# A vision tower on one core: scores in four 32-row quarters over four PSUM banks, and the norm weight of the last stage applied when turned gelu rows are evicted

## The chip, the core and the metric

The kernel runs on one core of one Trainium2 chip, in one launch. Its engines, each with its own queue of instructions in program order, are TensorE (PE, with its weight loads shown as PEld), VectorE (DVE), ScalarE (ACT), GpSimd (POOL) and SyncE (SP, which issues DMAs). Matrix products land in PSUM, eight banks of 512 float32 per partition, and are read from there by VectorE and ScalarE. The metric is the device time of the launch in microseconds, the median of several runs; lower is better.

## The reference

32 images of 96 x 96 x 3 are cut into 36 patches of 16 x 16 x 3; with two class tokens there are S = 38 tokens of D = 256 features. Then four residual blocks:

```python
h = patches @ W.T + b, class token, pos_embed; second class token in front
h = h + attn0(ln(h))       # 16 heads of 16, rope, causal softmax, @ Wo.T
h = h + moe(ln(h))         # 8 experts, top 2: sum_e gate_e * (x @ w_in[e].T @ w_out[e].T)
h = h + attn1(ln(h))       # 16 heads, no mask; every head's weights applied to 8 retrieval values,
                           #   a softmax over the 8 mixes them; @ Wf.T; then ln, relu MLP 256-512-256
h = h + ffn(ln(h))         # below
```

```python
h = x @ absmean(W_fc).T            # ternary weights: -1, 0, 1; 256 -> 1024
h = gelu(h)
h = layernorm(h, ln_w, ln_b)       # (h - mu) * rsqrt(var + eps) * ln_w + ln_b
return h @ absmean(W_proj).T       # ternary, 1024 -> 256
```

## The kernel before

The 1216 tokens are worked in T = 11 tiles of R = 114 rows (G = 3 images of 38 tokens); the last tile overlaps the one before. Every tile goes through four stages: a (patches, first attention), c1 (gate and experts), c2 and c3 (second attention and its MLP), d (the ternary block: d0 and d1 norm and first product, d2 gelu norm and projection). All order is written out by hand, engine by engine: straight lists of calls such as `c2_scores(2)`, and three hardware loops. The loop of stage a runs t = 2 to 7 and also multiplies each expert's two matrices together (`combine`). The middle loop runs `c_step(i)` for i = 5 to 10 and works on five tiles at once: c1 of i and i - 1, c2 of i - 2, the mixing of i - 3 and c3 of i - 4. The last loop runs `d_step(i)` for i = 4 to 10 with up to four tiles in hand; before it stands a straight list of what is left of c2 and c3 for tiles 9 and 10, with the first d calls between. Engines wait for each other through semaphores (`wait_ge`), each engine in its own order.

Precise products: an operand is split into a high part in float32r (one pass of the array) and a low part, the remainder; `mm3` (L1806 to L1810) multiplies high x high, high x low and low x high. So an eviction of a turned operand is a ScalarE copy to the high part (`turn_hi`, `d2_hi`) and a VectorE subtraction to the low part (`turn_lo`, `d2_lo`). Where one side is exact in the high part, as ternary weights are, two products do (`d1_fc`, L2163 and L2164). The projection of stage d has `ln_w` multiplied into its weights ahead of the loop (`proj_hi`, `proj_lo`: `pw_h`, `pw_l`), so it needs three (L2184); the mean is taken off by `ncs`, the column sums of those weights (`proj_sums`), and `ln_b` goes in by `bw` (`proj_bias`).

Scores of all 16 heads of three images are computed by block structure: `q_exp` holds q of one image with zeros around it, `k_exp` holds k of every head of a group in its 16 rows and zeros elsewhere, built by VectorE with the mask `hmask` (`a1_k`, `c2_k`, L1038 and L1264). Rows 0 to 63 and 64 to 127 of the array work on different banks of `score` (L1873). The softmax takes a maximum over both banks (L1044), subtracts it (L1050), takes three exps (L552), and `turn_p` (L1891) turns the 16 weights of 114 x 114 in four groups into two banks, `tb[0]` and `tb[1]`; ScalarE (L560), in stage a also VectorE (L1059), evicts each group to `pt`, and the group after next waits for that.

PSUM before: `bank0` to `bank2`, two banks of `score`, `tb0`, `tb1`, `bz`. The two `tb` banks also take turned x2, q and k, the products for q, k and v of stage c2, the output projection of stage a and, in stage d, the projection.

## Time and profile before

| what | value |
|---|---|
| median of three runs | 553.65 us (553.48 to 555.54) |
| profiled execution | 550.58 us, of which the span of the profile is 548.8 |
| granted TensorE clock over the span | 0.993 of full speed |
| instructions | 12145 |
| middle loop (six turns) | 289.8 to 415.7 us |
| from there to the end | 133.1 us |

The profile is one execution. Busy times of a group may overlap its neighbours; a record's duration is longer than its spacing from the next, since products are pipelined. A float32 product shows as two records, each of all its columns. A waiting time counts only where the waiting engine is the bound.

### The profile page before, as it was taken

To read this page: it belongs to the slowest core of one execution; us is meant where nothing else is said; L and a number is where in the kernel's file an instruction comes from. 1 tells how busy PE (TensorE), PEld (TensorE's weight loads), DVE (VectorE), ACT (ScalarE), POOL (GpSimd) and SP (SyncE) were. 2 spreads that over 40 slices of the span, in tenths; PEclk is the share of its full clock that TensorE was granted. 3 is DMA by queue.
4 is the path that set the end of the run, shared out by engine and by line. 5 is a ranking of instruction groups with operands and counts; after the bars stand their busy time and mean duration, and the time that the engine had idled before them with its cause. 6 is when DMAs were issued, how large, how long until landed. Compare 5 with 4: busy or idle time off the path is not lost.

```text
span 548.8 us, 12145 instructions
## 1 busy us (share of the span) xinstructions
PE 506.9 (92%) x3902; PEld 426.6 (78%) x3902; DVE 375.6 (68%) x943; ACT 272.9 (50%) x634; POOL 190.5 (35%) x257
## 2 busy tenths in 40 slices
PE   8989999999998878989999999999999989889996
PEld 7878877887877656667778888888888768678885
...
DMA packets 10990, 29.62 MB, mean 54 GB/s; under 512 B 2192, under 2 KB 3408, under 8 KB 10704
## 3 DMA queue, kind: packets, MB, share of 16 engines
...
q8 instruction: 17, 0.28, 0.2%
q14 instruction: 13, 0.11, 0.1%
...
## 4 chain that ended last, share of the span: by engine, by line
PE 42%; DVE 6%; issue 5%; ACT 3%; POOL 1%; DVEq 1%; POOLq 0%; ACTq 0%
PE score L2069 6%; PE tb L1808 3%; PE score L1873 3%; PE bz L2099 3%; PE tb L1810 3%; PE tb L1809 3%; PE bank L1810 3%; PE bank L1809 3%; PE bank L1808 3%; PE tb L1891 2%; PE bz L2081 2%; PE bz L1822 1%; PE bz L1808 1%; DVE we_h L1438 1%; PE tb L1822 1%
## 5 line engine op out<-in xcount | busy, mean ns | idle before, releaser
L383 POOL TENSOR_TENSOR h<-h,scaled 114x256 f32 (+1 forms) x88 | 69.1, 785 | 49.9 <-ACT scaled L686 43.3
L335 POOL TENSOR_TENSOR small<-small,half 114x1 f32<-114x1 f32 x44 | 25.8, 586 | 136.5 <-DVE small L969 136.5
L552 ACT ACTIVATE p_exp<-sc,cst 114x608 f32<-114x608 f32 x66 | 48.2, 795 | 25.6 <-DVE sc L1050 25.6
L1923 PE MATMUL bz<-ebuf 128*128 128x256 f32 x256 | 58.7, 382 | 0.0
L560 ACT ACTIVATE pt<-tb 114x456 f32<-114x456 f32 x66 | 34.6, 556 | 36.0 <-PE tb L1891 36.0
L1923 PEld LDWEIGHTS bz<-ebuf 128*128 128x128 f32 x256 | 47.7, 192 | 5.9
L1891 PE MATMUL tb<-cst,p_exp 114*114 114x114 f32 x352 | 44.0, 266 | 6.1 <-ACT pt L560 3.3
L2069 PE MATMUL score<-v,pt 114*114 114x137 f32 x352 | 48.9, 282 | 0.3 <-ACT o L653 0.3
L686 ACT ACTIVATE scaled<-bank,gl 114x256 f32<-114x256 f32 x88 | 39.0, 473 | 17.3 <-PE bank L1810 6.2
L1891 PEld LDWEIGHTS tb<-cst,p_exp 114*114 114x114 f32 x352 | 35.2, 134 | 15.1 <-ACT pt L560 6.7
L2069 PEld LDWEIGHTS score<-v,pt 114*114 114x114 f32 x352 | 44.1, 178 | 2.1 <-issue 0.4
L1873 PE MATMUL score<-k_exp,q_exp 64*114 64x152 f32 x528 | 40.6, 298 | 0.9 <-DVE k_exp L1264 0.8
L1873 PEld LDWEIGHTS score<-k_exp,q_exp 64*114 64x114 f32 x528 | 35.2, 175 | 7.0 <-issue 6.9
L1808 PE MATMUL bank<-we_h,xth 128*114 128x512 f32 x88 | 38.2, 434 | 0.1
L1809 PE MATMUL bank<-we_l,xth 128*114 128x512 f32 x88 | 35.0, 398 | 0.0
L1810 PE MATMUL bank<-we_h,xtl 128*114 128x512 f32 x88 | 34.9, 397 | 0.0
L346 POOL TENSOR_TENSOR o<-o 114x512 f32<-114x512 f32 x11 | 14.0, 1274 | 59.5 <-DVE o L1030 59.5
L653 ACT ACTIVATE o<-score 114x411 f32<-114x411 f32 (+1 forms) x66 | 31.2, 480 | 2.9 <-PE score L2069 2.0
L509 ACT ACTIVATE xth<-bank 128x228 fp32r<-128x228 f32 x33 | 11.8, 358 | 35.8 <-PE bank L1822 35.8
L1808 PE MATMUL tb<-wa,we_h 128*114 128x256 f32 x88 | 25.7, 292 | 2.5 <-DVE we_h L1438 2.1
L1044 DVE TENSOR_REDUCE smax<-score 114x16 f32<-114x608 f32 x22 | 17.3, 786 | 13.0 <-PE score L1873 12.9
L757 ACT ACTIVATE we_h<-score 128x456 fp32r<-128x456 f32 x22 | 11.1, 550 | 28.5 <-PE score L2175 28.5
...
## 6 DMA issues: line engine op xcount, KB each, us to landing
...
```

The costliest lines, as they stand in the source:

```text
L383: gp.tensor_tensor(h[0:R, t, :], h[0:R, t, :], scaled[0:R, e % 4, :], ALU.add).then_inc(moe_acc, 1)
L552: act.activation(p_exp[0:R, :, b * S:(b + 1) * S], sc[0:R], ACT.Exp, bias=cst[0:R, CB + b:CB + b + 1], scale=SCALE).then_inc(exps, 1)
L560: act.activation(pt[0:R, 4 * g:4 * g + 4, :], tb[g % 2][0:R, 0:4 * R].rearrange("p (h r) -> p h r", h=4), ACT.Copy).then_inc(pt_odd if g % ...
L653: act.activation(o1[0:R, h0:h0 + k, :], score[0:R, g % 2, 0:k * VE].rearrange("p (h d) -> p h d", h=k), ACT.Copy).then_inc(pv1_out, 1)
L686: act.activation(scaled[0:R, e % 4, :], bk[1 + e // 2 % 2][0:R, (e % 2) * D:(e % 2 + 1) * D], ACT.Copy, scale=gl[0:R, 7, e:e + 1]).then_in ...
L1808: pe.matmul(dst, lh, rh_, start=first, stop=False)
L1809: pe.matmul(dst, lh, rl_, start=False, stop=False)
L1810: return pe.matmul(dst, ll, rh_, start=False, stop=last)
L1873: last = pe.matmul(score[0:R, i, f * HQ * S:(f + 1) * HQ * S], q_exp[rows64, f].rearrange("p b x -> p (b x)")[:, b * R:(b + 1) * R], k_exp ...
L1891: last = pe.transpose(tb[g % 2][0:R, i * R:(i + 1) * R], p_exp[0:R, 4 * g + i, :], cst[0:R, CI:CI + R])
L1923: last = pe.matmul(bz[:, m * D:(m + 1) * D], ebuf[:, 0, c * D + m * P:c * D + (m + 1) * P], ebuf[:, 1, c * D:(c + 1) * D], start=(c == 0 a ...
L2069: last = pe.matmul(score[0:R, g % 2, i * VE:(i + 1) * VE], pt[0:R, place(h0 + i), :], v1[0:R, :], start=True, stop=True)
```

## The change

Scores. `score` has four banks; `tb[0]` and `tb[1]` are now its third and fourth. The head groups are halved (HQ = 2), `k_exp` and `hmask` are half as wide, and a score call has 24 products of 76 columns on four groups of 32 rows, each into its own bank, in place of 12 of 152 on two groups of 64. The causal mask is written by four products of 152 columns instead of two of 304. Maximum and subtraction read four banks with the same number of elements and operations. Since a score call overwrites `tb`, the output projection of stage a goes to the second half of `bank2` (but for the last tile), with waits on that bank's other reader, and in c2 the v product comes ahead of q and k.

Last stage. `d2_hi` multiplies by `ln_w` as it copies, one operation per chunk of 128 hidden units (the weight is then a value per partition): 8 of 114 columns instead of 2 of 456. `d2_lo` does the same with a multiply and subtract, 8 instead of 2. The projection uses the ternary weights themselves and needs two products per chunk. `proj_hi`, `proj_lo`, `lnw_halves` and `lnw_low` are gone; the column sums are computed in float32 from `ln_w` spread over 114 columns (`weight_wide`, `proj_sums`).

Order. The lists of all engines are written anew, and the last loop is written out, call by call, between what is left of c2 and c3.

```diff
     f, i, j = h // HF, h % HF // HQ, h % HQ
-    return i * HF + f * HQ + j
+    return i * HB + f * HQ + j
 
 
...
-        score = ctx.enter_context(nc.psum_tensor("score", [P, 2, 512], F32))
-        tb = [ctx.enter_context(nc.psum_tensor(f"tb{i}", [P, 512], F32)) for i in range(2)]
+        score = ctx.enter_context(nc.psum_tensor("score", [P, 4, 512], F32))
+        tb = [score[:, 2 + i, :] for i in range(2)]
+
+        def wo_place(t):
+
+            return tb[0][0:R, 0:D] if isinstance(t, int) and t == T - 1 else bk[2][0:R, D:2 * D]
...
-                    act.activation(gth[:, 4 * q:4 * q + 4, :], score[:, q, 0:4 * R].rearrange("p (c r) -> p c r", c=4),
-                                   ACT.Copy).then_inc(gT_hi, 1)
...
+                    for c in range(4):
+                        k = 4 * q + c
+                        last = act.activation(gth[:, k, :], score[:, q, c * R:(c + 1) * R], ACT.Copy, scale=lnwc[:, k:k + 1])
+                    last.then_inc(gT_hi, 1)
...
-            s = score[0:R, :, 0:HF * S].rearrange("p f (h j) -> p f h j", j=S)
+            s = score[0:R, :, 0:HB * S].rearrange("p f (h j) -> p f h j", j=S)
...
-                    V.tensor_tensor(sc[0:R, f * HF:(f + 1) * HF, :], s[:, f],
-                                    smax[0:R, f * HF:(f + 1) * HF].unsqueeze(2).broadcast_to([R, HF, S]),
-                                    ALU.subtract).then_inc(shifted, 1)
+                    two_banks = slice(2 * f * HB, 2 * (f + 1) * HB)
+                    top = smax[0:R, two_banks].rearrange("p (i h) -> p i h", i=2)
+                    V.tensor_tensor(sc[0:R, two_banks, :].rearrange("p (i h) j -> p i h j", i=2), s[:, 2 * f:2 * f + 2],
+                                    top.unsqueeze(3).broadcast_to([R, 2, HB, S]), ALU.subtract).then_inc(shifted, 1)
...
+            def weight_wide():
+                dve.wait_ge(pt_mm, 8 * T)
+                dve.wait_ge(lnw_in, 16)
+                V.tensor_copy(lnwr, lnwc[:].unsqueeze(2).broadcast_to([P, HC, R])).then_inc(widened, 1)
...
-                V.tensor_scalar(ncs[0:R], tb[0][0:R, 0:D], -1.0, None, ALU.mult).then_inc(bw_ready, 1)
+                V.tensor_scalar(ncs[0:R], tb[1][0:R, D:2 * D], -1.0, None, ALU.mult).then_inc(bw_ready, 1)
...
-                    V.tensor_tensor(gtl[:, 4 * q:4 * q + 4, :], score[:, q, 0:4 * R].rearrange("p (c r) -> p c r", c=4),
-                                    gth[:, 4 * q:4 * q + 4, :].bitcast(F32), ALU.subtract).then_inc(gT_lo, 1)
+                    for c in range(4):
+                        k = 4 * q + c
+                        last = V.scalar_tensor_tensor(gtl[:, k, :], score[:, q, c * R:(c + 1) * R], lnwc[:, k:k + 1],
+                                                      gth[:, k, :].bitcast(F32), ALU.mult, ALU.subtract)
+                    last.then_inc(gT_lo, 1)
...
+                since(dve, done, t)
+                dve.wait_ge(g_stat, 4 * t + 4)
...
             def a1_v(t):
                 since(pe, v0_ready, t)
+                since(pe, res0, t - 1)
...
-                    for i in range(2):
-                        pe.matmul(score[0:R, i, 0:HF * S], idb[0:R, 0:R], cmask[0:R], start=True, stop=False)
+                    for i in range(4):
+                        pe.matmul(score[0:R, i, 0:HB * S], idb[0:R, 0:R], cmask[0:R], start=True, stop=False)
...
-                        for i in range(2):
-                            rows64 = slice(i * P // 2, (i + 1) * P // 2)
+                        for i in range(4):
+                            rows32 = slice(i * P // 4, (i + 1) * P // 4)
                             last = pe.matmul(score[0:R, i, f * HQ * S:(f + 1) * HQ * S],
-                                             q_exp[rows64, f].rearrange("p b x -> p (b x)")[:, b * R:(b + 1) * R],
-                                             k_exp[rows64, f, :, b * S:(b + 1) * S],
+                                             q_exp[rows32, f].rearrange("p b x -> p (b x)")[:, b * R:(b + 1) * R],
+                                             k_exp[rows32, f, :, b * S:(b + 1) * S],
                                              start=(not causal and b == 0),
...
                 pe.wait_ge(oT_lo, t + 1)
-                product(tb[0][0:R, 0:D], xth[1], xtl[1], wa, A_O, D, (0, D)).then_inc(wo_mm, 1)
+                pe.wait_ge(v0_ready, min(t + 2, T) if isinstance(t, int) else t + 2)
+                product(wo_place(t), xth[1], xtl[1], wa, A_O, D, (0, D)).then_inc(wo_mm, 1)
...
             def c2_v(t):
-                pe.wait_ge(q_ready, 2 * (t + T) + 2)
+                pe.wait_ge(t2["lo"], t + 1)
                 product(tb[0][0:R, 2 * R:2 * R + W2], xth[1], xtl[1], wc, C_V, W2, (0, W2)).then_inc(v1_mm, 1)
 
             def c2_qT(t):
                 pe.wait_ge(qk1_out, t + 1)
+                pe.wait_ge(v1_ready, 2 * t + 2)
                 turned(tb[0][:, 0:2 * R], qk_rows[:, 0:D]).then_inc(qkT1_mm, 1)
...
             def c_step(i):
+                c2_pv(i - 3, (0, 1))
                 c2_x(i - 2)
-                c2_pv(i - 3, (0, 1))
                 c3_att(i - 4)
-                c2_pv(i - 3, (2, 3))
+                c2_pv(i - 3, (2,))
                 c3_wf(i - 4)
+                c2_pv(i - 3, (3, 4))
+                c1_moe(i - 1, (2,))
+                c2_pv(i - 3, (5,))
+                c2_v(i - 2)
+                c3_x(i - 4)
                 c2_qk(i - 2)
-                c2_pv(i - 3, (4,))
-                c1_moe(i - 1, (2,))
+                c1_moe(i - 1, (3,))
+                c1_x(i)
                 c2_qT(i - 2)
                 c2_kT(i - 2)
-                c2_pv(i - 3, (5,))
-                c1_x(i)
-                c3_x(i - 4)
-                c1_moe(i - 1, (3,))
+                c3_r1(i - 4)
                 c2_scores(i - 2)
-                c3_r1(i - 4)
+                c3_r1T(i - 4)
                 c1_gate(i)
-                c2_v(i - 2)
...
-                    pe.matmul(tb[0][0:R, 0:D], ones_r[:], pw_h[c], start=(c == 0), stop=False)
-                    last = pe.matmul(tb[0][0:R, 0:D], ones_r[:], pw_l[:, c, :], start=False, stop=(c == HC - 1))
+                    last = pe.matmul(tb[1][0:R, D:2 * D], lnwr[:, c, :], projt[:, c, :].bitcast(F32), start=(c == 0), stop=(c == HC - 1))
...
                 pe.wait_ge(gT_lo, 2 * t + 2)
-                since(pe, done, t)
+                since(pe, centred, t)
                 for c in range(HC):
-                    last = mm3(tb[0][0:R, 0:D], gth[:, c, :], gtl[:, c, :], pw_h[c], pw_l[:, c, :], c == 0, c == HC - 1)
+                    pe.matmul(tb[0][0:R, 0:D], gth[:, c, :], projt[:, c, :], start=(c == 0), stop=False)
+                    last = pe.matmul(tb[0][0:R, 0:D], gtl[:, c, :], projt[:, c, :], start=False, stop=(c == HC - 1))
                 last.then_inc(proj_mm, 1)
...
+            d2_turn(6, (0,))
+            d2_proj(5)
             c3_r1T(10)
+            d2_turn(6, (1,))
+            d1_fc(7, (0, 1))
+            d1_x(8)
+            d2_proj(6)
+            d2_turn(7, (0, 1))
             c3_r2(10)
-            with pe.Fori(4, T) as i:
-                d_step(i, 0, 3)
-            for i in range(T, T + 3):
-                d_step(i, i - T + 1, 3)
```

TensorE, middle loop, from before the turned weights (L1891, tb) to its end, before. L1808 to L1810 in bank are an expert pair, L2099 is r2, ISA and REGISTER_ALU are waits and counters of the loop.

```order
L1882 ISA
L1891 MATMUL tb<-cst,p_exp 114x114 x8
L1808 MATMUL bank<-we_h,xth 114x512
L1809 MATMUL bank<-we_l,xth 114x512
L1810 MATMUL bank<-we_h,xtl 114x512
L1808 MATMUL bank<-we_h,xth 114x512
L1809 MATMUL bank<-we_l,xth 114x512
L1810 MATMUL bank<-we_h,xtl 114x512
L117 REGISTER_ALU
L1891 MATMUL tb<-cst,p_exp 114x114 x8
L2097 ISA
L2099 MATMUL bz<-wr,x_raw 114x256 x4
```

The same place after (L1989 are the turned weights, L1905 to L1907 the expert pair, L2200 r2):

```order
L2198 ISA
L2200 MATMUL bz<-wr,x_raw 114x256 x4
L1980 ISA
L1989 MATMUL score<-cst,p_exp 114x114 x8
L118 REGISTER_ALU
L1989 MATMUL score<-cst,p_exp 114x114 x8
L1905 MATMUL bank<-we_h,xth 114x512
L1906 MATMUL bank<-we_l,xth 114x512
L1907 MATMUL bank<-we_h,xtl 114x512
L1905 MATMUL bank<-we_h,xth 114x512
L1906 MATMUL bank<-we_l,xth 114x512
L1907 MATMUL bank<-we_h,xtl 114x512
```

The expert pair stood between two halves of eight turns and now stands behind both; r2 has moved ahead of them.

TensorE around the last r2 (L2099), before; L2175 turns gelu rows, L2163 and L2164 are the first product of stage d:

```order
L1809 MATMUL bz<-wc,xth 114x512
L1810 MATMUL bz<-wc,xtl 114x512
L1822 MATMUL bz<-cst,raw 128x114 x4
L2099 MATMUL bz<-wr,x_raw 114x256 x4
L2357 UNCONDITIONAL_BRANCH
L2357 ISA
L2175 MATMUL score<-cst,ebuf 128x114 x8
L2158 REGISTER_ALU
L117 ISA
L2163 MATMUL bank<-wa,xth 114x512
L2164 MATMUL bank<-wa,xtl 114x512
```

After (r2 is L2200, L2276 turns gelu rows, L2286 and L2287 are the projection, L2264 and L2265 the first product):

```order
L2286 MATMUL score<-wa,we_h 114x256
L2287 MATMUL score<-wa,we_h 114x256
L2276 MATMUL score<-cst,ebuf 128x114 x8
L2200 MATMUL bz<-wr,x_raw 114x256 x4
L2264 MATMUL bank<-wa,xth 114x512
L2265 MATMUL bank<-wa,xtl 114x512
L2264 MATMUL bank<-wa,xth 114x512
L2265 MATMUL bank<-wa,xtl 114x512
L1919 MATMUL bank<-cst,xn 128x114 x2
```

Before, the last loop starts right behind r2; after, r2 of tile 10 stands between tiles 7 and 8 of stage d.

VectorE around the last addition to h of c3 (L1326), before; L1438 is d2_lo, L1452 d2_out:

```order
L1429 BN_AGGR small<-small 114x2
L1433 TENSOR_TENSOR qvs<-small,cst 114x2
L1452 SCALAR_TENSOR_TENSOR h<-x,qvs,h 114x256
L1326 TENSOR_TENSOR h<-bz,h 114x256
L1798 UNCONDITIONAL_BRANCH
L117 REGISTER_ALU
L974 ISA
L974 TENSOR_SCALAR xn<-h,small 114x256
L1437 ISA
L1438 TENSOR_TENSOR we_h<-score,we_h 128x456
L1437 REGISTER_ALU
L1438 TENSOR_TENSOR we_h<-score,we_h 128x456
```

After (the addition is L1327, L1444 is d2_lo, L1455 d2_centre, L1461 d2_out):

```order
L1455 SCALAR_TENSOR_TENSOR x<-scaled,qvs,score 114x256
L1444 SCALAR_TENSOR_TENSOR we_h<-score,lnwc,we_h 128x114 x4
L1327 TENSOR_TENSOR h<-bz,h 114x256
L1444 SCALAR_TENSOR_TENSOR we_h<-score,lnwc,we_h 128x114 x4
L1461 SCALAR_TENSOR_TENSOR h<-x,qvs,h 114x256
L960 BN_STATS small<-h 114x6
L965 BN_AGGR small<-small 114x2
L981 TENSOR_TENSOR xtl<-bank,xth 128x228
L969 TENSOR_SCALAR small<-small 114x1
```

The addition, which lay ahead of the last loop, now lies within the low parts of tile 7, and each low part is four small operations a half.

## Rows read from the trace of the kernel before

**Rows 1.** The page, part 1: busy time, share and instructions of each engine.
```profile
PE 506.9 (92%) x3902; PEld 426.6 (78%) x3902; DVE 375.6 (68%) x943; ACT 272.9 (50%) x634; POOL 190.5 (35%) x257
```

**Rows 2.** Windows (length, busy us (x) of PE, PEld, DVE, ACT, POOL, PEclk, DMA).
```profile
289.80:415.70 125.90, 125.90 (x890) 107.10 (x889) 101.22 (x293) 91.59 (x234) 58.90 (x84) 1.00 0.00 0
415.70:548.80 133.10, 118.94 (x823) 101.72 (x821) 96.64 (x246) 72.57 (x165) 36.15 (x56) 1.00 0.04 10
500.74:518.94 18.20, 17.75 (x126) 15.68 (x126) 15.54 (x40) 7.33 (x16) 5.42 (x9) 1.00 0.07 19
```

**Rows 3.** Waits of TensorE: us in total, times, longest.
```profile
PE score L1868 <- DVE y L1069: 3.6, 3, 1.4
```

**Rows 4.** Groups by line and form, TensorE: xcount, busy us, mean ns, idle.
```profile
L1873 PE MATMUL score<-k_exp,q_exp 64*114 64x152 f32 x528 | 40.6, 298 | 0.9 <-DVE k_exp L1264 0.8
...
L2138 PE MATMUL tb<-wa,k_exp 128*114 128x256 f32 x16 | 3.6, 379 | 0.0
```

**Rows 5.** Timeline (start, us), TensorE: first stage, then one turn of the loop.
```profile
143.78 0.99 PE L1902 MATMUL score<-pt,scaled 114*32 114x114 f32 x32
...
362.85 1.82 PE L1873 MATMUL score<-k_exp,q_exp 64*114 64x152 f32 x24
364.60 0.49 PE L1808 MATMUL bz<-wc,xth 128*114 128x512 f32 x1
...
366.10 0.24 PE L1809 MATMUL bank<-wc,xth 128*114 128x8 f32 x1
366.19 0.24 PE L1810 MATMUL bank<-wc,xtl 128*114 128x8 f32 x1
...
369.04 0.95 PE L1891 MATMUL tb<-cst,p_exp 114*114 114x114 f32 x8
369.76 0.46 PE L1808 MATMUL bank<-we_h,xth 128*114 128x512 f32 x1
...
371.22 0.94 PE L1891 MATMUL tb<-cst,p_exp 114*114 114x114 f32 x8
```

**Rows 6.** Timeline, TensorE: turned weights in one piece, ahead of the loop.
```profile
285.92 0.96 PE L1891 MATMUL tb<-cst,p_exp 114*114 114x114 f32 x8
287.14 1.05 PE L1891 MATMUL tb<-cst,p_exp 114*114 114x114 f32 x8 [0.25 <-ACT pt L560]
288.02 1.89 PE L2099 MATMUL bz<-wr,x_raw 128*114 128x256 f32 x8
```

**Rows 7.** Timeline, all engines: one turn of the last loop.
```profile
506.81 0.37 PE L1808 MATMUL tb<-wa,we_h 128*114 128x256 f32 x1 [0.15 <-DVE we_h L1438]
...
509.61 0.28 PE L1810 MATMUL tb<-wa,we_h 128*114 128x256 f32 x1
...
510.32 0.99 ACT L757 ACTIVATE we_h<-score 128x456 fp32r<-128x456 f32 x2 [2.97 <-PE score L2175]
...
511.66 1.16 DVE L1438 TENSOR_TENSOR we_h<-score,we_h 128x456 fp32r<-128x456 f32 x2
```

**Rows 8.** Groups by line and form, VectorE.
```profile
L1264 DVE SCALAR_TENSOR_TENSOR k_exp<-tb,vec,cst 128x456 f32<-128x456 f32 x22 | 14.2, 687 | 4.3 <-PE tb L1822 4.3
...
L981 DVE TENSOR_TENSOR xtl<-bank,xth 128x228 fp32r<-128x228 f32 x33 | 12.9, 390 | 3.6 <-ACT xth L509 3.2
...
L1446 DVE SCALAR_TENSOR_TENSOR x<-scaled,qvs,tb 114x256 f32<-114x256 f32 x11 | 5.3, 479 | 7.1 <-PE tb L1810 7.1
...
L1273 DVE TENSOR_TENSOR qvs<-tb,cb 114x16 f32 x6 | 1.0, 165 | 0.0
```

**Rows 9.** Groups by line and form, ScalarE.
```profile
L675 ACT ACTIVATE x_raw<-bz,vec 128x114 f32<-128x114 f32 x44 | 12.2, 353 | 0.7 <-PE bz L1822 0.7
...
L748 ACT ACT_TABLE_LOAD x2 | 2.6, 1283 | 0.0
```

**Rows 10.** Timeline, VectorE: the wide bias, and the last r2.
```profile
458.20 0.62 DVE L1399 COPY k_exp<-vec 128x912 f32<-128x912 f32 x1
...
486.06 0.42 DVE L1326 TENSOR_TENSOR h<-bz,h 114x256 f32<-114x256 f32 x1 [3.44 <-PE bz L2099]
```

1141 lines of the change are left out of this document (623 added, 518 removed).

## The prediction

> **What bounds the kernel now.** I read the page first: TensorE is busy for 92% of the span, VectorE for 68% [rows 1]. Then the stretches. From 289.8 to 415.7 us (six turns of the middle loop) TensorE has no idle time at all, and from there to the end 14.2 of 133.1 us [rows 2]. In the last loop three turns, 500.74 to 518.94, have TensorE busy for 17.75 of 18.2 us and VectorE for 15.54 [rows 2]. So matmul time is the price almost everywhere, and a matmul removed is worth its spacing, as long as VectorE, at 85% in the last loop, doesn't take over. Of TensorE's waits the longest in total is one of 3.6 us on VectorE [rows 3].
>
> **Scores in quarters.** Before, a score call is 24 records (12 matmuls, two records each) on two 64-row groups. They last 298 ns on average, but the whole takes 1.75 us to the next product, 362.85 to 364.60 [rows 4, 5]: steps of two records, (1.82 - 0.29)/11.5 = 0.13 us a step, which is 304 columns at 2.4 GHz (granted clock 1.00 there [rows 2]). Afterwards it is 48 records of half the columns on four 32-row groups, twelve steps of four. Two things could set a step: the columns, 0.065 us, or the load of the stationary operand, which still has 114 columns. The trace shows that load by itself: products of 8 columns on a 114-column operand stand 0.09 us apart [rows 5], and I take 0.10. That four records can share one step is shown for column groups: 32 records of L1902 take 0.99 us, (0.99 - 0.26)/7.75 = 0.094 a step of four [rows 5]; for row groups it is shown for two only. At 0.10 a call saves 12 x 0.03 = 0.36 us; 22 calls, 7.9 us. Bounds: 0.065 a step (17 us saved) and 0.20, two turns of loads a step (18 us lost).
> The row says 0.10. The Trainium skill (TensorE: Matmul & The Clock Gate, LDWEIGHTS) says the same against this change: a load goes by its columns and not by its rows. Another of its pages (TensorEngine Tiling, Theoretical Speedup) promises up to four times for 32 rows where 64 rows have two; by that a step would be the 0.065 of the lower bound, a rival below.
> The causal mask of the first stage goes from two products of 304 columns, 0.13 each, to four of 152, each held by its load at 0.095: 11 x 0.12 = 1.3 us more.
> VectorE's k_exp products shrink from 456 to 228 elements, 0.69 to about 0.45 us each [rows 8]. This lies beside TensorE in the loops and is worth nothing there.
>
> **The two banks that become scores.** tb is now half of score. So a score call may start only when v, q and k have left tb; for that c2_v moves ahead of c2_qk, and c2_qT waits for v1_ready. Between c2_v and c2_qT stand twelve products of 512 columns (six of them take 1.46 us, 369.76 to 371.22 [rows 5]) and two pairs of transposes, 3.2 us; VectorE has seven operations of 0.17 to 0.48 us [rows 8], about 2.2, in it: no wait. Were it late, kT, r1 and the scores would be late with it. The softmax chain after the scores had 4.4 us of matmuls over it, 364.60 to 369.04 [rows 5], and has r1T, the gate, one expert pair and r2 now, about 4.1; I price that at nothing, since the loop shows no idle TensorE at 4.4, with 0.3 a turn as its bound.
> In the loop the four groups of turned weights now come in one piece, c2_turn_p(0..3), where before an expert pair stood between two and two. Split, a half takes 0.72 us, 369.04 to 369.76, so both 1.44 [rows 5]. In one piece, as already once before the loop, they take from 285.92 to 288.02 = 2.10 us, since the third waits for ScalarE to empty its bank [rows 6]. Six turns x 0.66 = 4.0 us lost. Bounds: 0 and 0.9 a turn.
>
> **First stage and the way into the loop.** 11 calls x (0.36 - 0.12) = 2.6 us and 3 x 0.36 = 1.1 us gained; the loop 6 x 0.36 = 2.2 us. The three waits, 3.6 us together, for the attention output ahead of scores 8 to 10 (L1868 behind y L1069) [rows 3] get a projection more over them (a1_v, 0.7 us), but a2_pv itself now waits for its turned weights; I take 1.0 us (0 to 3.6).
>
> **The last stage.** TensorE: the norm weight is now applied when the turned gelu rows are evicted, so d2_proj needs no low part of the weights and has 16 products, not 24. They stand 0.117 us apart (23 steps in 506.81 to 509.61, with 0.1 for the first) [rows 7]: 88 fewer, 10.3 us. The sums go from 16 such products to 8 of plain float, which take 3.6 us with their 16 records in proj_bias [rows 4]: 1.6 us more. Two score calls less 0.7. TensorE's 118.9 us of the stretch [rows 2] become 109.5.
> VectorE: d2_lo was two operations of 456 elements, 1.16 us for both [rows 7]; it is now eight of 114 with a scalar per partition. No row has it. The same form takes 0.687 us with 456 elements and 0.479 with 256 [rows 8], a slope of 1.03 ns, so 0.33 us for 114, less the 0.04 by which neighbours overlap: 0.29. Bounds: 0.165 (16 elements) and 0.39 (228) [rows 8]. 8 x 0.29 = 2.35, 1.19 more a tile, 13.1 us for eleven; less 1.0 for four k_exp, 0.6 more for the wide weight, as for the wide bias [rows 10]: 96.6 [rows 2] becomes 109.3 us. ScalarE's d2_hi goes from 0.99 a tile [rows 7] to 8 x 0.28 = 2.2, and two more table loads of 1.28 us come (gelu between exps) [rows 9]: at most 73 + 16 = 89 of 133 us, which hides.
> So TensorE and VectorE have the same 109 us. How much of it overlaps? The list written out instead of the loop puts the last tiles' attention tail between steps of the last stage. Before, VectorE waited 3.44 us for the last r2 at 486.06 [rows 10], with nearly 60 us of the last stage still to come. Now only fc 8 to 10, projections 7 to 10 and turns 8 to 10 stand behind c3_r2(10): 24 x 0.24 + 64 x 0.117 + 24 x 0.09 + 0.4 = 15.8 us. Ahead of it are 109.5 - 15.8 = 93.7 us of matmul, to which I add 6 of waits (under half of today's 14.2; two turned pieces are in it). Behind it VectorE is the bound: 28 small operations (8.1), six row statistics (3.9), nine centre and out steps (4.3), the rest 3.2, together 19.5 us; and the last tile is a chain in which VectorE waits for two projections and a turn, 4 more: 23.5. Sum 93.7 + 6 + 23.5 = 123.2, as against 133.1: 9.9 us gained. Bounds: 115 (TensorE at 95%) and 134 (below).
>
> **Sum.** 2.6 + 1.1 + 2.2 + 1.0 + 9.9 - 4.0 = 12.8 us. The profiled execution took 550.6 us, span 548.8, which is 3.1 below the median of 553.65; the same difference on the median gives 540.8 us.
>
> **Rivals.**
> The four groups do not run together (slower). If the loads of four row groups pass two at a time, a step is 0.20 us and a call takes 2.6 instead of 1.75. For it: only two are shown. Against: four column groups. 22 x 12 x 0.10 = 26.4 us on the forecast: 567 us. It decides from 0.15 us a step, where the sum is zero.
> VectorE bounds the last stage. If a small operation costs 0.39, VectorE has 109.3 + 8.8 = 118 us; at the 88% that it may reach beside its waits (85% in today's loop) that is 134, the gain of the last stage is gone: 551.5 us.
> All of it is collected. ScalarE frees the banks in time and TensorE keeps 95% in the last stretch: 4.0 + 8.2 more, 528.6 us. Against: TensorE's idle 14.2 us of today [rows 2].
> The step is bound by columns (what TensorEngine Tiling promises): 22 x 12 x 0.035 = 9.2 us more, 531.6 us. Against: the spacing of the 8-column products.
> The new order of the loop waits for its exps or banks by 1.5 us a turn, and the way in by 3: 553 us.
>
> **How the numbers follow.** The forecast has 0.52, with a range of its own from 535 to 546; slower by the loads 0.07; VectorE 0.14; all collected 0.13; columns 0.06; the loop's waits 0.08. The range 531 to 552 leaves out the slower case, most of the loop's waits and half of the all collected one, 0.2 together. Half a per cent, about what a measurement of this kernel tells from no change, is 2.8 us: faster means below 550.9. The forecast, all collected, columns and half of VectorE's give 0.78, and 0.02 of the loop's: 0.80. Same: the other half and 0.04: 0.11. Slower: 0.07 and 0.02, 0.09.
>
> **What would show it.** Score calls of 48 records in 1.4 us, four of them every 0.10. In the loop a turn of about 21.3 us (125.9 / 6 = 20.98 now [rows 2]), with a wait on pt inside the turned weights. Small operations of 0.33 us on VectorE; VectorE over 88% busy in the last 60 us, and the stretch from the end of the loop 10 us shorter. Wrong would be a score call over 2 us, a loop turn under 20.7 or over 22, or last-stage tiles that still come 6 us apart with VectorE idle.

## The result: 550.06 us, and the profile after

| | before | changed |
|---|---|---|
| median of the first comparison | 553.65 us (5 runs) | 550.06 us (5 runs) |
| ratio | 1 | 0.9939, 95% interval 0.9915 to 0.9964 |
| the same kernel in a later series | 552.86 us (17 runs) | 548.25 us (12 runs), ratio 0.9922 (0.9891 to 0.9953) |
| profiled execution, its span | 550.58, 548.8 us | 552.54, 550.5 us |
| mean granted clock of that run | 0.993 | 0.971 |

The changed kernel is 0.6 to 0.8% faster. The forecast was 540.8, 2.3% faster: the direction is right, the size is not. The profiled run of the changed kernel is even 1.7 us longer than that of the kernel before, and its clock is lower. So the page comes first, and then its clock.

Page of the changed kernel, part 1 (answers to [rows 1]) and the row of the granted clock (tenths of full speed in 40 slices):

```profile
PE 501.6 (91%) x4364; PEld 420.5 (76%) x4364; DVE 377.3 (69%) x1009; ACT 281.7 (51%) x684; POOL 201.4 (37%) x257
...
PEclk9998999999998899899999999999999999999997
```

A slice is 13.8 us. The eights lie at 41 to 55, at 165 to 193 and at 220 to 234 us, the last two between the first stage and the middle loop, and the seven at the end. First windows of the changed kernel there (columns as in [rows 2]), then windows of the kernel before:

```profile
50.00:58.00 8.00, 7.79 (x66) 6.74 (x67) 2.04 (x5) 2.55 (x4) 2.38 (x2) 0.57 0.40 133
...
174.00:181.00 7.00, 5.71 (x23) 5.01 (x24) 2.51 (x6) 3.00 (x6) 0.87 (x1) 0.54 0.26 53
191.00:195.00 4.00, 4.00 (x20) 3.78 (x19) 1.69 (x5) 2.19 (x3) 0.00 (x0) 0.62 0.00 0
218.00:225.00 7.00, 7.00 (x63) 5.78 (x57) 2.42 (x10) 2.39 (x5) 0.00 (x0) 0.51 0.00 0
...
540.00:550.50 10.50, 3.76 (x16) 3.45 (x16) 3.90 (x14) 1.65 (x7) 1.24 (x2) 0.61 0.06 19
```

```profile
15.00:19.00 4.00, 4.00 (x15) 3.34 (x14) 2.77 (x6) 0.38 (x1) 1.12 (x2) 0.57 0.96 338
50.00:58.00 8.00, 7.18 (x53) 6.14 (x53) 2.60 (x7) 2.56 (x4) 2.38 (x2) 1.00 0.52 173
166.00:181.00 15.00, 12.32 (x119) 10.11 (x121) 11.21 (x27) 4.14 (x8) 8.31 (x9) 1.00 0.41 142
213.00:217.00 4.00, 4.00 (x26) 3.16 (x23) 2.59 (x8) 0.53 (x2) 0.00 (x0) 0.57 0.00 0
```

Half the clock is 1.2 GHz, full 2.4. Summed over windows of 1 us within the span, as twice what is missing from 1.00, the changed kernel's run has 32.2 us at 1.2 GHz, 23.9 of them ahead of the loop, and the run before 7.7. (The recorded expectations have 9.7 for it and 18.5 for e8's run; these sums take in time behind the end of the span, and within it they are 7.7 and 16.1.)

**The scores came out as forecast.** One call is 48 records, and from its start to the next product 328.65 to 330.02 = 1.37 us, where it was 1.75 [rows 5]: steps of four at 0.10 us. Timeline of TensorE in one turn of the changed kernel's middle loop (start, us):

```profile
328.65 1.44 PE L1971 MATMUL score<-k_exp,q_exp 32*114 32x76 f32 x48
330.02 0.61 PE L1919 MATMUL bz<-cst,raw 114*128 114x114 f32 x4
...
332.45 1.89 PE L2200 MATMUL bz<-wr,x_raw 128*114 128x256 f32 x8
334.30 0.99 PE L1989 MATMUL score<-cst,p_exp 114*114 114x114 f32 x8
335.63 1.05 PE L1989 MATMUL score<-cst,p_exp 114*114 114x114 f32 x8 [0.33 <-ACT pt L574]
```

The turned weights in one piece now take from 334.30 to the next product at 336.44, 2.14 us (forecast 2.10), with the wait for ScalarE inside. The six score calls of the loop start 21.56 us apart (307.09 to 414.88 in five turns); before it was 20.98.

**The last stage.** Groups by line and form, then the waits of TensorE from 455 us on (us in total, times, longest); they answer to [rows 7]:

```profile
L2286 PE MATMUL score<-wa,we_h 128*114 128x256 f32 x88 | 23.6, 303 | 6.2 <-DVE we_h L1444 6.2
L755 ACT ACTIVATE we_h<-score,lnwc 128x114 fp32r<-128x114 f32 x88 | 23.1, 371 | 17.6 <-PE score L2276 11.0 <-PE score L2287 6.5
L1444 DVE SCALAR_TENSOR_TENSOR we_h<-score,lnwc,we_h 128x114 fp32r<-128x114 f32 x88 | 22.8, 325 | 2.1 <-ACT we_h L755 2.0
L2287 PE MATMUL score<-wa,we_h 128*114 128x256 f32 x88 | 22.7, 293 | 0.0
```

```profile
PE score L2286 <- DVE we_h L1444: 6.2, 6, 2.9
PE bz L1919 <- DVE x L974: 1.6, 1, 1.6
```

And a window, with VectorE's 19.24 of 20 us:

```profile
500.00:520.00 20.00, 18.51 (x127) 15.83 (x126) 19.24 (x68) 13.70 (x44) 5.29 (x9) 1.00 0.05 16
```

A small operation lasts 0.325 us by itself, and four in a row 1.01 to 1.07, 0.26 each. The longest wait, 2.94 us, is that of the last tile, which has nothing beside it: the turn, eight small ScalarE operations, eight small VectorE operations, and then 16 products at half clock. Timeline of all engines there:

```profile
538.98 0.94 PE L2276 MATMUL score<-cst,ebuf 114*128 114x114 f32 x8
...
539.57 2.08 ACT L755 ACTIVATE we_h<-score,lnwc 128x114 fp32r<-128x114 f32 x8 [2.75 <-PE score L2276]
...
541.80 1.01 DVE L1444 SCALAR_TENSOR_TENSOR we_h<-score,lnwc,we_h 128x114 fp32r<-128x114 f32 x4
...
542.86 0.56 PE L2286 MATMUL score<-wa,we_h 128*114 128x256 f32 x1 [2.94 <-DVE we_h L1444]
543.12 0.15 DVE L1437 TENSOR_TENSOR qvs<-small,cst 114x2 f32<-114x2 f32 x1
543.22 0.42 PE L2287 MATMUL score<-wa,we_h 128*114 128x256 f32 x1
```

**Where the time is, by stages.** The loop's turn begins with `c2_pv` in the changed kernel and with `c2_x` before. Their first products, changed and before:

```profile
294.40 1.57 PE L2170 MATMUL score<-v,pt 114*114 114x137 f32 x12
```

```profile
289.75 0.36 PE L1822 MATMUL tb<-cst,x 114*128 114x114 f32 x2
```

A turn has its scores 12.3 us behind this start, so the sixth ends at 307.09 - 12.3 + 6 x 21.56 = 424.2 us. (The first turn has 12.7 up to its scores, with 0.4 us of small gaps.) So the way to the loop takes 294.4 us (289.8 before), the loop 129.8 (125.9), and 126.3 us are left behind it (133.1): 4.6 and 3.9 us lost, 6.8 gained, which is the 1.7 of the spans but for rounding. The forecast had 4.7 gained, 1.8 lost, 9.9 gained. The loss ahead of the loop is the surprise.

The last r2, `c3_r2(10)`, cuts the stretch behind the loop in two, as the forecast did. It begins at 521.63 and VectorE adds its result from 523.56 on:

```profile
521.63 1.89 PE L2200 MATMUL bz<-wr,x_raw 128*114 128x256 f32 x8
```

So 99.3 us lie ahead of its end (forecast 93.7 + 6 = 99.7) and 27.0 behind it (forecast 23.5), in which VectorE is busy for 17.3 us, 64%, and TensorE waits three times for the small operations (0.7, 1.1 and 2.9 us):

```profile
523.50:550.50 27.00, 18.41 (x117) 15.59 (x115) 17.27 (x58) 10.03 (x33) 4.97 (x8) 0.85 0.07 20
```

**A place for it.** Timeline of ScalarE, GpSimd, VectorE and TensorE at 172 us of the changed kernel:

```profile
172.56 1.91 ACT L623 ACTIVATE raw<-ebuf 128x2048 f32<-128x2048 f32 x1 [4.17 <-POOL wc L352]
...
174.47 0.34 ACT L523 ACTIVATE xth<-bank 128x228 fp32r<-128x228 f32 x1
174.84 0.39 DVE L981 TENSOR_TENSOR xtl<-bank,xth 128x228 fp32r<-128x228 f32 x1 [2.42 <-ACT xth L523]
...
175.29 0.77 PE L1905 MATMUL bank<-wa,xth 128*114 128x512 f32 x1 [3.10 <-DVE xtl L981]
```

L623 is `tern_sum(0)`, the absolute sum over the fc weights. The new ScalarE list has it ahead of `a1_x(8)`; the old one had it much later. It waits for GpSimd, runs 1.9 us and reads its sum out in 0.2, and only then is the turned x of tile 8 evicted. TensorE stands for 3.10 us (0.88 before), and within this wait its clock falls to half. The window 174 to 181 above shows what follows.

### The profile page after: what moved, and what is told of

Same layout as the page of the kernel before. It is cut to its first block, busy times and chain, and to the rows that moved or that the text cites. A ratio compares the mean times of both kernels' runs of the same rounds, so it can differ in the third digit from the quotient of the medians.

```text
span 550.5 us, 12974 instructions
## 1 busy us (share of the span) xinstructions
PE 501.6 (91%) x4364; PEld 420.5 (76%) x4364; DVE 377.3 (69%) x1009; ACT 281.7 (51%) x684; POOL 201.4 (37%) x257
## 3 DMA queue, kind: packets, MB, share of 16 engines
q1 hardware_dynamic: 10960, 29.15, 15.9%
## 4 chain that ended last, share of the span: by engine, by line
PE 65%; issue 15%; DVE 8%; ACT 7%; POOL 3%; DMA 1%; POOLq 0%; SPq 0%; ACTq 0%; DVEq 0%
PE score L2170 8%; PE bz L2022 6%; PE bank L1905 6%; PE bank L1907 6%; PE bank L1906 6%; PE score L1971 4%; PE score L1989 4%; PE bz L2200 3%; DVE we_h L1444 3%; PE score L2286 2%; ACT pt L574 2%; PE score L2287 2%; PE score L1919 2%; PE bz L1919 2%; PE bz L2182 2%
## 5 line engine op out<-in xcount | busy, mean ns | idle before, releaser
L383 POOL TENSOR_TENSOR h<-h,scaled 114x256 f32 (+1 forms) x88 | 70.4, 800 | 53.5 <-ACT scaled L700 46.9
L566 ACT ACTIVATE p_exp<-sc,cst 114x608 f32<-114x608 f32 x66 | 48.2, 795 | 23.9 <-DVE sc L1052 23.9
L2022 PE MATMUL bz<-ebuf 128*128 128x256 f32 x256 | 60.3, 389 | 0.0
L574 ACT ACTIVATE pt<-score 114x456 f32<-114x456 f32 x66 | 34.8, 549 | 42.1 <-PE score L1989 42.0
L1989 PE MATMUL score<-cst,p_exp 114*114 114x114 f32 x352 | 45.2, 270 | 7.2 <-ACT pt L574 6.0
L1989 PEld LDWEIGHTS score<-cst,p_exp 114*114 114x114 f32 x352 | 34.9, 135 | 18.4 <-ACT pt L574 10.8
L1905 PE MATMUL bank<-we_h,xth 128*114 128x512 f32 x88 | 37.2, 423 | 0.0
L1907 PE MATMUL bank<-we_h,xtl 128*114 128x512 f32 x88 | 35.0, 398 | 0.0
L1971 PEld LDWEIGHTS score<-k_exp,q_exp 32*114 32x114 f32 x1056 | 30.3, 184 | 5.8 <-issue 4.8
L1971 PE MATMUL score<-k_exp,q_exp 32*114 32x76 f32 x1056 | 33.6, 273 | 0.9 <-DVE k_exp L1265 0.8
L755 ACT ACTIVATE we_h<-score,lnwc 128x114 fp32r<-128x114 f32 x88 | 23.1, 371 | 17.6 <-PE score L2276 11.0
L340 POOL TENSOR_TENSOR small<-small,half 114x2 f32<-114x2 f32 x11 | 17.0, 1542 | 37.6 <-DVE small L1196 37.6
L1905 PE MATMUL bank<-wa,xth 128*114 128x256 f32 (+1 forms) x64 | 23.8, 372 | 7.6 <-DVE xtl L981 5.0
L1044 DVE TENSOR_REDUCE smax<-score 114x16 f32<-114x608 f32 x22 | 17.3, 787 | 18.1 <-PE score L1971 18.1
```

The lines of the kernel that those rows point to most:

```text
L383: gp.tensor_tensor(h[0:R, t, :], h[0:R, t, :], scaled[0:R, e % 4, :], ALU.add).then_inc(moe_acc, 1)
L566: act.activation(p_exp[0:R, :, b * S:(b + 1) * S], sc[0:R], ACT.Exp, bias=cst[0:R, CB + b:CB + b + 1], scale=SCALE).then_inc(exps, 1)
L574: act.activation(pt[0:R, 4 * g:4 * g + 4, :], tb[g % 2][0:R, 0:4 * R].rearrange("p (h r) -> p h r", h=4), ACT.Copy).then_inc(pt_odd if g % ...
L1905: pe.matmul(dst, lh, rh_, start=first, stop=False)
L1907: return pe.matmul(dst, ll, rh_, start=False, stop=last)
L1971: last = pe.matmul(score[0:R, i, f * HQ * S:(f + 1) * HQ * S], q_exp[rows32, f].rearrange("p b x -> p (b x)")[:, b * R:(b + 1) * R], k_exp ...
```

## The experiments

Each was compared with the kernel before, on the same chip; the changed kernel's own ratio is 0.9927, the mean of its two series weighted by runs. Clock is the median of the granted clock of its runs.

| run | median us | ratio (95%) | clock |
|---|---|---|---|
| changed kernel | 550.06, 548.25 | 0.9939, 0.9922 | 0.979 |
| e1 sum later | 546.34 | 0.9867 (0.9832 to 0.9901) | 0.980 |
| e2 turned weights split | 552.38 | 0.9983 (0.9957 to 1.0009) | 0.978 |
| e3 waits filled | 548.45 | 0.9901 (0.9864 to 0.9938) | 0.985 |
| e4 wide evictions | 541.40 | 0.9786 (0.9748 to 0.9824) | 0.980 |
| e5 scores in halves | 558.75 | 1.0123 (1.0085 to 1.0161) | 0.983 |
| e6 low product twice | 561.85 | 1.0142 (1.0090 to 1.0195) | 0.976 |
| e7 low part on GpSimd | 561.85 | 1.0161 (1.0119 to 1.0203) | 0.977 |
| e8 e1 and fillers | 543.70 | 0.9843 (0.9804 to 0.9883) | 0.988 |
| e9 e8, half pairs between | 543.54 | 0.9826 (0.9793 to 0.9859) | 0.989 |
| e10 e8, end filled too | 542.08 | 0.9798 (0.9766 to 0.9830) | 0.997 |
| e11 e9 and e10 | 542.07 | 0.9797 (0.9764 to 0.9831) | 0.997 |
| e13 kernel before, filled | 549.40 | 0.9946 (0.9921 to 0.9972) | 0.997 |
| e14 changed kernel, filled | 543.63 | 0.9842 (0.9811 to 0.9874) | 0.998 |

**e1, the sum later.**

```diff
-            tern_sum(0)
             a1_x(8)
 ...
             a1_pt(8, (0, 2))
+            tern_sum(0)
             a1_v(9)
```

> The changed kernel with one ScalarE step moved: the absolute sum of the fc weights (L623, 2.1 us) no longer stands ahead of the eviction of the turned x of tile 8, but behind the first p evictions of tile 8, where the kernel before has it. Theory 1 (a step of the new ScalarE list is in the way): in the profiled run the eviction at 174.47 waited for this sum, which itself waited for POOL's split of the weights until 172.47, and TensorE stood still for 3.1 us and then ran 6.8 us at half clock. Moved, the wait falls to about 0.9 us (as before the change), the half-clock stretch at 174 to 181 is gone or shorter, and the kernel takes 2.2 (the wait alone) to 5.5 us less: 544.5 to 548 us. Rival (the way in is bound by POOL's splits of x and of the weights, or by the attention chain): the wait comes back at another place and the time stays within 1 us of 550.

Measured 0.9867, which is 0.6% or 3.3 us below the changed kernel; its interval lies below that of the first series and overlaps the second's by 0.001. The wait is the 0.88 us of before. TensorE in e1:

```profile
172.94 0.48 PE L1905 MATMUL bank<-wa,xth 128*114 128x512 f32 x1 [0.88 <-DVE xtl L981]
```

Its profiled run still has 3.4 us at half clock from 173 on and 23.5 in all. Theory 1 stands within its range; the half-clock stretch became shorter and did not go. From the mask of scores 7 to that of scores 8 (L1966) it takes 15.9 us where the changed kernel took 18.9.

**e2, the turned weights in two pieces.**

```diff
-                c2_turn_p(i - 2, (0, 1, 2, 3))
+                c2_turn_p(i - 2, (0, 1))
                 c1_moe(i, (1,))
+                c2_turn_p(i - 2, (2, 3))
```

> The changed kernel with the middle loop's turned weights in two pieces, an expert pair between them (the order is r2, groups 0 and 1, expert pair 1, groups 2 and 3). Theory 1 (a wait moves, it does not go): the four groups take 1.5 us instead of 2.14, but the products with v at the turn's start then stand right behind the last group and wait for its eviction by 0.5 to 0.9 us; a turn stays at 21.4 to 21.7 us and the kernel within 1.5 us of 550. Rival (the 0.63 us a turn was free to save): a turn of 20.9 us, the kernel 3.8 us faster, 546.

A turn became 22.16 us, 0.6 more, and the kernel 3 us slower. Waits of TensorE in four turns of e2; the wait has only moved, and grown:

```profile
PE score L2170 <- ACT pt L574: 4.3, 4, 1.1
```

Both misjudged it; theory 1 had the place right and the size too small (0.5 to 0.9 us a wait, a turn of at most 21.7).

**e3, waits filled.**

```diff
             a1_x(8)
+            pe.wait_ge(we_lo, E)
+            warm(12)
             a1_qk(8)
 ...
+            warm(4)
             scores(8, True)
```

and likewise 4 ahead of scores 9, 7 ahead of scores 10 (`warm(n)`: n products of 128 x 128 into `bz`).

> The changed kernel with idle time of TensorE on the way into the loop filled by products that nobody reads (128x128 of ones into the bank bz, which is free there): 12 ahead of the q and k products of tile 8, 4 ahead of scores 8 and 9, 7 ahead of scores 10. Theory 1 (the half clock follows the idle time and costs more than it): TensorE keeps the granted clock at 1.00 from 170 to 230 (now 17 us of it at half clock); what it ran at half clock takes half the time, up to 8 us less, of which waits for other engines give some back: 543 to 547 us. Rival A (the half clock follows the narrow score products, not the waits): the drops stay at about 174, 191 and 218 and the time is 549 to 552. Rival B (at full clock the waits behind simply grow, since VectorE and ScalarE set the pace there): clock 1.00, but the time within 1.5 us of 550.

The stretches at 174 and 191 are at full clock now:

```profile
166.00:181.00 15.00, 13.50 (x143) 11.97 (x141) 9.62 (x23) 6.27 (x12) 5.35 (x6) 1.00 0.41 150
186.00:195.00 9.00, 8.27 (x98) 6.91 (x98) 5.48 (x14) 3.57 (x6) 0.55 (x1) 1.00 0.00 0
218.00:228.00 10.00, 8.07 (x71) 5.82 (x72) 4.52 (x11) 2.99 (x7) 2.01 (x3) 0.66 0.00 0
```

That speaks for idle time and against the narrow products, which are all still there (rival A). One run does not show it for 191, since e1 and e12, without fillers, have no stretch there either. It does for 174, over all runs: of the eight profiled runs of the changed kernel and its variants without fillers, seven have a half-clock stretch that begins at 172 to 175 us (all but e7), and of the six with fillers none has. A wait of 1.7 us ahead of the turned weights 10 was not filled here, and behind it the clock fell at 220. Only 1.4 us were gained: inconclusive between theory 1 and rival B.

**e4, wide evictions.** This one leaves the norm weight out, so its result is not the reference's; it is a measure of what the small operations cost.

```diff
-                    for c in range(4):
-                        k = 4 * q + c
-                        last = act.activation(gth[:, k, :], score[:, q, c * R:(c + 1) * R], ACT.Copy, scale=lnwc[:, k:k + 1])
-                    last.then_inc(gT_hi, 1)
+                    act.activation(gth[:, 4 * q:4 * q + 4, :], score[:, q, 0:4 * R].rearrange("p (c r) -> p c r", c=4),
+                                   ACT.Copy).then_inc(gT_hi, 1)
```

and the same for `d2_lo`, as a subtraction.

> The changed kernel with the norm weight left out at the eviction of the turned gelu rows: two wide ScalarE operations of 456 elements instead of eight of 114, and two wide VectorE operations instead of eight (the rest of the last stage as it is). VectorE saves (8 x 0.26 - 2 x 0.58) x 11 = 10 us of work, ScalarE about 1.1 us a tile. Theory 1 (the small operations are on the path of the last tiles: TensorE waits 6.2 us for them): the waits of the projection for VectorE fall under 2.5 us and the kernel takes 3 to 6 us less, 544 to 547. Rival (TensorE's products set the last stage, the waits come back elsewhere): within 1.5 us of 550.

1.4% or 7.8 us faster, more than theory 1 had: TensorE's waits for this step fell from 6.2 to 1.6 us.

```profile
PE score L2281 <- DVE we_h L1440: 1.6, 1, 1.6
```

**e5, the scores in halves.**

```diff
-HB = H // 4
-HQ = H // 8
+HB = H // 2
+HQ = H // 4
 ...
-                        for i in range(4):
-                            rows32 = slice(i * P // 4, (i + 1) * P // 4)
+                        for i in range(2):
+                            rows32 = slice(i * P // 2, (i + 1) * P // 2)
```

> The changed kernel with the scores alone taken back to two halves of 64 rows in two of the four banks (24 records a call, two mask products of 304 columns, k_exp of 456 elements); order, banks and last stage stay as changed. Theory 1 (a score call saves 0.37 us and the mask costs 0.12 more, and TensorE sets the pace wherever they stand): 22 x 0.37 - 11 x 0.12 = 6.8 us slower than the changed kernel's 550, 557. Rival (in the stages with waits the shorter call only lengthens the wait behind it, since VectorE's maximum, ScalarE's exponentials and the turns come at their own time): 3 us slower or less, 550 to 553. A turn of the middle loop: 21.56 + 0.37 = 21.9 us by the first, 21.6 by the second.

2.0% or 10.8 us slower: the quarters are worth more than the 6.8 us of theory 1. A call takes 1.75 us again, and a turn of the loop 22.08, 0.52 more. On top of the 6.8 come 4.0 us. In the profiled run TensorE's waits for the exponentials, for the wider `k_exp` and for the attention outputs are 2.6, 1.8 and 4.7 us, where the changed kernel has 1.1, 0.8 and 3.9: 3.3 us more, outside the loop. In the loop 0.14 us a turn stay without a place.

**e6, the low product twice.** The low part is added twice, which changes the result by that small part only.

```diff
+                    pe.matmul(tb[0][0:R, 0:D], gtl[:, c, :], projt[:, c, :], start=False, stop=False)
                     last = pe.matmul(tb[0][0:R, 0:D], gtl[:, c, :], projt[:, c, :], start=False, stop=(c == HC - 1))
```

> The changed kernel with the product of the low part issued twice in each chunk of the projection (24 products a tile as before the change, where it has 16; the low part is so added twice, which is all that differs in the result). It gives back what the last stage saves on TensorE: 8 x 0.117 x 11 = 10.3 us. Theory 1 (TensorE sets the last stage): 8 to 10 us slower than the changed kernel, 558 to 560. Theory 2 (VectorE and ScalarE's small operations set it, as the 8.5 us say that went with wide operations): the products fill waits, and it costs 4 us or less, 551 to 554.

2.1% or 11.9 us slower. The waits for the small operations are the same 6.2 us, so the products came on top of them: TensorE sets the last stage and the small operations add to it. Theory 1 here and theory 1 of e4 both hold; I had put them as rivals.

**e7, the low part on GpSimd** (on e1): VectorE multiplies by the weight laid wide into `pt`, ScalarE rounds, and

```diff
+                    gp.tensor_tensor(gtl[:, 4 * q:4 * q + 4, :], pt[:, 4 * q:4 * q + 4, :],
+                                     gth[:, 4 * q:4 * q + 4, :].bitcast(F32), ALU.subtract).then_inc(gT_lo, 1)
```

> The kernel of the first experiment (sum moved) with the eviction of the turned gelu rows done otherwise, the norm weight kept: VectorE multiplies 456 elements at a time by the weight laid wide (2 operations a tile, about 0.62 us each, where eight take 2.1), ScalarE rounds them to the high part (2 of 0.5), GpSimd subtracts for the low part (2 of about 1.1 us by its rows of 296 and 684 elements). VectorE has 9 us less in the last stage. Theory 1 (VectorE's small operations bound the last stage): 4 to 8 us less than that kernel's 546.3, so 538 to 542. Rival (the chain over three engines is longer and TensorE waits for GpSimd instead): 545 us or more.

The rival won by far, 3.0% slower than e1. GpSimd's operation takes 1.2 us, and TensorE waits for it in nine tiles:

```profile
PE score L2302 <- POOL we_h L427: 18.1, 9, 4.1
```

**e8 to e11, more fillers, and another split.** e8 is e1 with fillers at nine places on the way in; e9 adds

```diff
-                c2_turn_p(i - 2, (0, 1, 2, 3))
-                c1_moe(i, (1,))
+                c2_turn_p(i - 2, (0, 1))
+                c1_moe(i, (1,), (0,))
+                c2_turn_p(i - 2, (2, 3))
+                c1_moe(i, (1,), (1,))
```

and e10 adds `warm(6)` ahead of `a1_turn(10)` and 2, 4 and 11 ahead of the projections 7, 9 and 10.

> The kernel of the first experiment (sum moved) with idle time of TensorE filled by products nobody reads, at more places than in the third: 4 ahead of scores 1, 3 ahead of the q and k products of tile 8, 4 ahead of scores 8 and 9, 7 ahead of scores 10, 3 ahead of each of the attention outputs 7 to 10. Theory 1 (the half clock at 50 to 57 and 173 to 218 follows idle time of TensorE; held at full clock the way in takes less): half-clock time before the middle loop falls from 17 us to under 7, and the kernel takes 2 to 5 us less than 546.3: 541 to 544. Rival (as in the third, where 10 us of half clock less brought only 2 us: the engines behind set the pace and the fillers cost what they save): 545 to 548.

> The kernel of e8 with the middle loop's turned weights in two pieces again, but only half an expert pair (three of its six products, 0.7 us) between them and the other half behind the second piece, so that both the bank and the products with v have something to wait behind. Theory 1 (the one piece costs 0.63 us a turn for want of cover, and the second experiment lost it again because its cover stood at one place only): the wait of 0.33 inside the piece goes, the products with v wait 0.3 us or less, a turn takes 21.1 to 21.3 us instead of 21.56, and six turns give 1.5 to 3 us on e8's 543.7: 541 to 542. Rival (the eviction by ScalarE is late whatever stands between, since its queue is in another order): a turn of 21.5 or more, 543 to 547.

> The kernel of e8 with three more waits of TensorE filled by unread products: 6 ahead of the turned weights 10 (a wait of 1.7 us for the exponentials, after which a half-clock stretch began at 216), 2, 4 and 11 ahead of the projections 7, 9 and 10 (waits of 0.7, 1.1 and 2.9 us; half clock from 537 to the end). Theory 1 (half clock follows idle time): half-clock time falls from 18.5 to under 8 us; what TensorE runs at half clock after 537 (about 5 us of products) takes half, and the time is 2 to 4 us under 543.7: 540 to 542. Rival (the end is a chain through VectorE and ScalarE in which TensorE's clock matters little): 543 to 545.

> The edits of e9 and e10 together. If both theories hold, the gains add: 538 to 541. If neither, 543 to 546.

e8 gained 0.24% on e1, inside both intervals. In e9 a turn is 21.58 us, as ever: the wait left the piece and stands, 0.4 us a turn, ahead of the products with v (rival). e10 took the clock to 0.997, and is 1.3% or 7.1 us faster than the changed kernel. Its end is at full clock, as is all from 166 to 250:

```profile
166.00:250.00 84.00, 77.47 (x863) 64.00 (x862) 56.09 (x148) 38.63 (x83) 32.93 (x40) 1.00 0.08 27
...
530.00:543.70 13.70, 9.27 (x74) 8.51 (x72) 7.57 (x27) 3.76 (x13) 2.50 (x4) 1.00 0.08 23
```

Theory 1 of e10 is borne out at its weak end: 1.6 us below e8 by the medians, where it had 2 to 4, and with intervals that overlap. Its profiled run still has 10.2 us at half clock, all ahead of the loop, but it is the slowest of the seven, at a clock of 0.991; the other six have 0.997. e11 adds nothing to it. With 542.1 us e10 and e11 are the fastest kernels of the study that leave nothing of the computation out.

**e12, the changed kernel again.**

> The changed kernel itself, in the same series as its variants: 550 us (547.5 to 552.5), 0.990 to 0.997 of the kernel before. If it comes out under 547 or over 553, the differences of 2 to 4 us between it and its variants in other series are not to be read.

It came out near the first series: 548.25 us. Its profiled run has 19.5 us at half clock where the first had 32.2, and a span of 546.4 where the first had 550.5.

**e13 and e14, both kernels filled.** The clock differs between the kernels and from run to run, so both were brought near 1.00, e13 with fillers at ten places and e14 at thirteen.

> The kernel before the change, with idle time of TensorE filled by unread products at ten places: ahead of scores 1, the q and k products of tile 8, scores 8 to 10, the turned q of tiles 8 and 9, the turned weights 9 and 10 and the attention output 10. Its profiled run had 9.7 us at half clock, 3.4 of them at 213 and 3.4 at 15. Theory (the clock explains the spread of its runs, 5 us per 0.01, and half clock follows idle time): the median clock rises from 0.990 to 0.993 or more, and the time falls by 1 to 3 us, to 550 to 552. Rival (the clock of this kernel is set elsewhere): the fillers cost what they take, 553 to 555.

> The changed kernel with its idle time filled in the same way at fourteen places, those of e10, but the absolute sum left where the change puts it, with 12 products over its wait. Theory 1 (about 6 of the missing 9 us are clock): with both kernels near a clock of 0.995 the difference between them is 8 to 10 us, so 542 to 545 here. Rival (the missing time is waits and work, the clock only a sign of them): the difference to the filled kernel before stays at 3 to 5 us, 547 or more.

Before 549.40, changed 543.63: at nearly equal clock the change is worth 5.8 us (0.9842/0.9946 = 0.9895), with the fillers' own cost in it. That lies between the two theories. As the kernels are, it is worth 4.0 (0.9927). So of the 8.8 us that are missing from the forecast 12.8, the clock holds about 1.8 by this pair, and waits and work 7.0.

e14 is also e10 with the sum left where the change puts it (and 12 fillers over its wait instead of 3), both at full clock there. From the mask of scores 7 to that of scores 8, first e10, then e14:

```profile
169.07 0.43 PE L1966 MATMUL score<-cmask,idb 114*114 114x152 bf16 x4
183.93 0.47 PE L1966 MATMUL score<-cmask,idb 114*114 114x152 bf16 x4 [0.19 <-DVE y L1070]
```

```profile
165.96 0.43 PE L1966 MATMUL score<-cmask,idb 114*114 114x152 bf16 x4
182.52 0.47 PE L1966 MATMUL score<-cmask,idb 114*114 114x152 bf16 x4 [0.19 <-DVE y L1070]
```

That is 14.86 and 16.56 us: at full clock the misplaced sum costs 1.7 us. The medians of the two kernels are 1.6 us apart, the ratios 2.4.

## Why the prediction was right or wrong

In short: the score calls and the products of the last stage cost what was forecast. The gain on the way into the loop did not come, because the new ScalarE list puts a long step ahead of an eviction there; the loop lost twice what was forecast; the last tiles wait for the small operations; and the clock, which the sum did not have, took the rest.

The profiled run of e14 has nothing at half clock and that of e13 3.4 us ahead of the loop, so their way to the loop shows the change without its clock. What 3.4 us at half clock cost lies between nothing and 1.7 us, and the table has both ends. For the other two rows the run before stands, which has full clock there up to its last 2 us.

| step | forecast | e14 against before |
|---|---|---|
| to the loop's start | -4.7 | 286.2 against e13's 289.3: -3.1 to -1.4 |
| the loop, six turns | +1.8 | 416.1 - 286.2 = 129.9 against 125.9: +4.0 |
| behind the loop | -9.9 | 541.2 - 416.1 = 125.1 against 133.1: -8.0 |

**The step that failed is "First stage and the way into the loop"** (4.7 us gained), with 4.6 us lost in the profiled run and at most 3.1 gained at full clock. Its terms for the score calls held: a turn of the first stage's loop went from 19.71 to 19.48 us, as forecast. Its 1.0 us for the waits for the attention outputs did not come (3.9 us where [rows 3] has 3.6). And it never followed the new ScalarE list, where a step of 2.1 us had been moved ahead of the first eviction of the stretch: 1.7 us at full clock (e14 against e10), 3.3 with what its wait does to the clock (e1). e11 has the sum moved back and the same 3.4 us at half clock as e13: its loop begins at 285.3, 4.1 us earlier than e13's. So with the sum out of the way 4.1 of the 4.7 are there, and what is left, 0.6, is less than the 1.0 of the waits.

**The clock was no term at all.** The sum took TensorE's time as if it ran at 2.4 GHz throughout, which [rows 2] show only for the stretches they cover. The changed kernel runs at a median clock of 0.979 (17 runs), that before at 0.989 (62 runs of the four later series). Within each kernel the runs lie near a line: before, from 549.29 us at 0.996 to 556.67 at 0.981; changed, from 544.63 at 0.988 to 552.54 at 0.971. Lines fitted through all of them give 4.5 us for 0.01 of clock before and 3.7 changed. By these the difference in clock would cost about 4 us; at 0.990 the lines stand at 552.6 and 544.8 us, 7.8 apart. e13 and e14 are only 5.8 apart. e13 lies on the line of its kernel (549.4 at 0.997). e14 lies 2 us above the line of its own, continued to 0.998, which none of the 17 runs reaches. That its fillers cost these 2 us is one possibility, and was not tried. So at equal clock the change is worth 5.8 to 7.8 us, and the clock holds 1.8 to 3.8 of the 8.8 that are missing. In the two profiled runs of the changed kernel the loop begins at 294.4 and 291.2 us, and in e14 at 286.2; so a single profiled run can lose 5 to 8 us ahead of the loop, for the most part to the clock.

**The loop**: scores -0.38 a turn (forecast -0.36), and the turned weights 2.14 us where two pieces took 1.50, +0.64 (forecast 0.66), of which 0.33 are the wait for ScalarE. On top come 0.34 us that no term had, in steps of the timeline that stand at other places now: the products with wf take 0.89 us instead of 0.67, those of r2 1.85 instead of 1.73. Together this is the 0.58 that a turn grew, where the sum had 0.30; the difference is 1.7 us over six turns, and 0.4 more come in the first turn. In e2 and e9 the wait for ScalarE's eviction only moved, so neither split made the piece cheaper.

**The last stage** was right in mechanism: 16 products a tile are worth what was said (e6: 8 products a tile cost 11.9 us, 10.3 forecast), the small operations last 0.325 by themselves (forecast 0.33) and 0.26 in a row (forecast 0.29), and wide ones, without the weight, take 7.8 us less (e4). TensorE is busy for 109.7 us of the stretch (forecast 109.5), VectorE for 101.6 (forecast 109.3). The stretch came out at 126.3 in the profiled run and 125.1 in e14, with 123.2 forecast. What went wrong there is the tail. Ahead of the last r2's end 99.3 us passed in both runs (forecast 99.7); behind it 27.0 and in e14 25.8, where the forecast had 23.5 with VectorE as the bound and 4 us of its waits. VectorE was busy for 17.3 us of it. The last tiles are chains of a turn, ScalarE's and VectorE's small operations and the projection, with 4.7 us of TensorE's waits in them, 2.94 of these in the last tile, and behind that products at half clock.

**The rivals.** Four groups together: yes, 0.10 us a step; neither the slower rival's 0.20 nor the columns' 0.065. By the Trainium skill (TensorE: Matmul & The Clock Gate, LDWEIGHTS) a load goes by its columns and not by its rows. The trace agrees as to the rows, with 0.10 us a step of four 32-row products on 114 columns, where [rows 5] have 0.09 for 128 rows and the same 114 columns; these rows do not test the columns. VectorE as the bound of the last stage: half true. From 500 to 520 us it is busy for 19.24 of 20 us, but e6 shows that TensorE's products count in full, and an operation costs 0.26 in a row, not the 0.39 of the rival. The last rival, the new order waiting on the way in and in the loop, is the nearest to what happened; it had 0.08.

**What would show it**: score calls of 1.4 us, yes; turns of 21.3, 21.56; small operations of 0.33, yes; VectorE over 88% in the last 60 us, no, 79%; the stretch behind the loop 10 us shorter, 6.8. One of the signs of being wrong came in part: the last three projections start 5.8 and 5.9 us apart (531.18, 537.00, 542.86), with VectorE idle for a third of the time.
